# One counter for the activated x channels, one for the B and C rows of a Mamba block

## The chip, the cores and the metric

The kernel runs on one core of a Trainium2 chip. The metric is the time of one execution on the device in microseconds (us), as the median of several runs. Before the change: 3848.72 us, the median of 3 runs (3846.72 to 3849.55).

## What is computed

The input x is 64 batches of 256 x 256 float32. Two layers follow, each a graph attention and a feed-forward block, each on a layer norm of x and added to x.

```
x = x + L0_gnn(layernorm(x), adj)      # two dense layers, two attentions, ELUs
x = x + L0_ffn(layernorm(x))           # top-k routing, GELU, scatter back
x = x + L1_gnn(layernorm(x), adj)      # one masked attention, ELU
x = x + L1_ffn(layernorm(x))           # the Mamba block
```

The change lies in the Mamba block:

```
z, xBC, dt = split(x @ W_in)
xBC  = silu(conv_b + causal convolution of xBC over 4 taps)
xh, Bmat, Cmat = split(xBC, [512, 576])          # 512 x channels, 64 B rows, 64 C rows
xdt  = xh * dt                                   # dt = softplus(dt + dt_bias)
Y    = einsum(C, B, exp(segsum(dt * A)), xdt) + xh * D
Y    = Y * silu(z) ; RMS norm ; @ W_out @ W_lin + b_lin
```

## The kernel before

**Tiling.** All is float32. A batch is one 256 x 256 tile, held as two halves of 128 rows (U = 2). Matrices that go through TensorE are kept transposed, channels on partitions: the convolved channels are five tiles of 128 x 256 in `acc`, the first four (KI = 4) the 512 x channels, the fifth the 64 B rows and the 64 C rows. The eight PSUM banks are A0 to A2 (first attention), Q0, Q1 (router and second attention) and M0 to M2 (Mamba).

**Order of the work.** The 64 batches are pipelined. The table `STEPS` gives each of the five engines a written-out list of steps with a lag for each: in turn t a step of lag 5 works on batch t - 5. The prologue and the drain are unrolled, the turns between are one hardware loop. An engine does its instructions in order, and engines meet in semaphores alone, each of which is a counter: `then_inc(S["name"], 1)` on an instruction raises it when the instruction is done, `wait_ge(S["name"], b)` holds an engine's queue until the counter has reached b, the number of the batch.

**The place of the change.** The steps of the Mamba block that bear on it, with the engine and the lines:

- `m_silu` on ScalarE takes tanh of all five tiles of `acc` into `th` (L738). `m_silu` on VectorE then makes silu times two out of it, in three operations: L1010 for the four x tiles, in place (`xc` is another name of `acc`), L1012 for the B rows into `bT`, L1014 for the C rows into `cT`. The last one raises `xc_ready`.
- `m_xrow` on TensorE transposes `xc` back to rows, eight 128 x 128 transposes (L1339) into M2 and M0. ScalarE's `m_xrow` copies them to `xr` (L749), GpSimd's makes `xdt = xr * dt` (L564), which `m_y` on TensorE reads (L1353).
- `m_cb` on TensorE, right behind `m_xrow` in its list, multiplies `bT` and `cT` (L1332, L1333). VectorE masks the product into `cb` (L1030).
- `m_xbc_a` on ScalarE writes the first tap of the convolution of the next batch into `acc` (L708), and before that waits until the batch before is done with it (`before(act, S["xc_ready"], b)`).

On TensorE the list around it reads: `q_ffn1.1` (L1257), `a_mlp1.0` and `a_mlp1.1` (L1129, sixteen matmuls), `m_xrow`, `m_cb`, `a_fc.0` and `a_fc.1` (L1140), `q_ffn2` (L1264), a few small steps, `m_y` (L1353), `a_att` (L1160). On VectorE: ... `b_elu_c` (L904), `b_x1` (L921, L927), `q_gelu_a` (L963), `m_silu`, `g_x3` (L933), statistics, `m_cb` (L1030), `a_fc` (h, L807), `m_norm`, `q_ffn2` (L974, the GELU product, whose tanh is L704 on ScalarE). ScalarE's decays of the Mamba block are L760 and L764.

Of the kernel before, what the change touches and what calls it, by code (L numbers as in the profile page):

```python
# [7 lines left out]
ALU = mybir.AluOpType  # L8
# [36 lines left out]
def gnn_ffn_mamba_kernel(nc, x, adj, mlp1_w, mlp1_b, mlp2_w, mlp2_b, W_fc, a_fc, W_hand, a_hand,  # L45
# [24 lines left out]
    with ExitStack() as ctx:  # L70
# [6 lines left out]
        def sem(name):  # L77
            return ctx.enter_context(nc.semaphore(name))
# [141 lines left out]
        def rows1(half, u, extra=0):  # L220
# [13 lines left out]
            wsum_ready w_ps wrow_ready rank_ready pick_ready sel_ps sel_ready  # L234
            up_ps ga_ready gsq_ready gq_ready gt_ready gl_ready yff_ps yff_ready sc_ps xs_ready
            x2_ready x3_ready
            xbc_ps acc_ready conv th_ready xc_ready
            dt_ps dt_a_ready dt_abs dt_e_ready dt_chain dt_ready dA_ps cumT_ready cumc_ps cumcol_ready
            cb_ps cb_ready z_ps tz_ready gz_ready xr_ps xr_ready xdt_ready fall_ready dec0_ready dec1_ready mix_ready
            y_ps ysum yg_ready sq_ready sq_half yss_ready ss_ps ms_ready da_ready rms_ready out_ps x3b_ready x4_ready"""  # L240
        S = {name: sem(name) for name in NAMES.split()}
# [214 lines left out]
        def nth(b, per, i):  # L456

            return b * per - (per - i)

        def before(eng, semaphore, b):  # L460

            if not (isinstance(b, int) and b < 2):
                eng.wait_ge(semaphore, b - 1)
# [115 lines left out]
        def _(act):  # L579
# [126 lines left out]
            def first_tap(k, src):  # L706

                return nc.scalar.activation(acc[:, k, :], src, ACT.Identity, bias=c_conv[:, k:k + 1],  # L708
                                            scale=w_conv[:, k, PAD:PAD + 1])

            def m_xbc_a(b):
                before(act, S["xc_ready"], b)
                act.wait_ge(S["xbc_ps"], nth(b, 3, 1))
                first_tap(4, M1[:, N:2 * N])
                nc.scalar.copy(bc_in[:, PAD:], M1[:, N:2 * N]).then_inc(S["acc_ready"], 1)

                if not (isinstance(b, int) and b < 2):
                    act.wait_ge(S["ysum"], nth(b, 2, 0))
                act.wait_ge(S["xbc_ps"], nth(b, 3, 2))
                first_tap(0, M2[:, 0:N])  # L720
                first_tap(1, M2[:, N:]).then_inc(S["acc_ready"], 1)
# [44 lines left out]
            def m_gated(b):  # L766
# [8 lines left out]
                b_att=elu_exp("b", A2), g_att=elu_exp("g", Q1), b_elu_b=b_elu_b, g_elu=g_elu,  # L775
                q_route=q_route, q_gather=q_gather, q_gelu_a=q_gelu_a, q_gelu_c=q_gelu_c,
                m_xbc_a=m_xbc_a, m_xbc_b=m_xbc_b, m_dt_exp=m_dt_exp, m_silu=m_silu, m_z=m_z,
                **parts("m_decay", m_decay, 2), m_xrow=m_xrow, m_gated=m_gated))

        @block.vector  # L780
        def _(v):
# [224 lines left out]
            def m_silu(b):  # L1006

                v.wait_ge(S["th_ready"], b)
                c = acc
                nc.vector.scalar_tensor_tensor(out=xc[:, 0:KI, :], in0=th[:, 0:KI, :], scalar=1.0, in1=c[:, 0:KI, :],  # L1010
                                               op0=ALU.add, op1=ALU.mult)
                nc.vector.scalar_tensor_tensor(out=bT[:], in0=th[0:DS, KI, :], scalar=1.0, in1=c[0:DS, KI, :],  # L1012
                                               op0=ALU.add, op1=ALU.mult)
                nc.vector.scalar_tensor_tensor(out=cT[:], in0=th[DS:, KI, :], scalar=1.0, in1=c[DS:, KI, :],  # L1014
                                               op0=ALU.add, op1=ALU.mult).then_inc(S["xc_ready"], 1)

            def m_scan(b):
                v.wait_ge(S["dA_ps"], b)
# [60 lines left out]
            def m_out(b):  # L1079
# [17 lines left out]
                b_x1=b_x1, g_x3=g_x3, q_route=q_route, q_rank=q_rank,  # L1097
                q_gelu_a=q_gelu_a, q_gelu_b=q_gelu_b,
                q_ffn2=q_ffn2, q_scatter=q_scatter, q_x2=q_x2, **parts("m_conv_b", m_conv_b, PAD), m_silu=m_silu,
                m_scan=m_scan,  # L1100
                m_cum_col=m_cum_col, m_cb=m_cb, m_gate=m_gate,
# [3 lines left out]
        def _(pe):  # L1105
# [221 lines left out]
                last.then_inc(S["cumc_ps"], 1)  # L1327

            def m_cb(b):
                pe.wait_ge(S["xc_ready"], b)  # L1330
                pe.wait_ge(S["cumcol_ready"], b)
                nc.tensor.matmul(M1[:, 0:N], bT[:, 0:P], cT[:, :], start=True, stop=True)  # L1332
                nc.tensor.matmul(M1[:, N:N + P], bT[:, P:], cT[:, P:], start=True, stop=True).then_inc(S["cb_ps"], 1)  # L1333
# [31 lines left out]
            def m_out(b):  # L1365
# [14 lines left out]
                g_att=att("g", Q1), q_route=q_route, q_gather=q_gather, **parts("q_ffn1", q_ffn1, 2),  # L1380
                q_ffn2=q_ffn2, q_scatter=q_scatter, m_xbc_a=m_xbc_a, m_xbc_b=m_xbc_b, m_z=m_z, m_da=m_da,
                m_cum_col=m_cum_col, m_cb=m_cb, m_xrow=m_xrow, **parts("m_y", m_y, 2), m_dt=m_dt, m_ss=m_ss, m_out=m_out))


# [23 lines left out]
```

## Time and profile before

| | before |
|---|---|
| median of 3 runs | 3848.72 us (3846.72 to 3849.55) |
| profiled execution: its own time | 3847.21 us |
| its span, first to last instruction | 3845.5 us |
| PE (TensorE matmul) busy | 3658.6 us, 95% |
| PEld (TensorE weight load) busy | 3166.9 us, 82% |
| DVE (VectorE) busy | 2966.9 us, 77% |
| ACT (ScalarE) busy | 2364.6 us, 61% |
| POOL (GpSimd) busy | 997.1 us, 26% |
| mean granted TensorE clock | 0.983 of full speed |

The profile is of one execution. Its times count from the first instruction of the program. A busy share is an average over the whole span; PE's matmuls are pipelined, and the ends of their rows are modelled, so that a row of a group can reach a little into the next. "M<-ident,acc" is an instruction that writes a tile M from tiles ident and acc; "x8" are eight of them merged into one row. What stands in brackets at the end of a row is how long the engine was idle before it, and which instruction it waited for.

### The profile page before, as it was taken

The numbers are of one execution on the slowest core, as the hardware profiler recorded it, in microseconds if no ns is written. First come the engines' busy times: TensorE is split into PE (matmuls) and PEld (weight loads), VectorE is DVE, ScalarE is ACT, GpSimd is POOL, SyncE is SP. The second block draws the span as 40 slices with busy tenths as digits, with TensorE's granted clock in tenths as the row PEclk, the third lists the DMA queues.
The fourth block names the chain that finished last, engine by engine and source line by source line (L and its number), as shares of the span: only waits on it lengthen the run. The fifth ranks groups of instructions, "written<-read, shape, count | busy, mean of one in ns | idle before, by whom it ended". The sixth has DMA issues, their size and how long they took to land.

```text
span 3845.5 us, 63918 instructions
## 1 busy us (share of the span) xinstructions
PE 3658.6 (95%) x21016; PEld 3166.9 (82%) x21016; DVE 2966.9 (77%) x7731; ACT 2364.6 (61%) x5314; POOL 997.1 (26%) x1817
## 2 busy tenths in 40 slices
PE   2789999999999999999999999999999999999985
PEld 2578888888888888888888888888888888888864
DVE  2358887887887888788787888878878788887875
ACT  1246666666666666666666666666666666666654
POOL 0012223223223222322322222232232222223222
PEclk9889999999999999999999999999999999999987
DMA  3000010010011001001001100100100110010000
GB/s 93 11 23 28 30 38 27 30 38 27 30 38 38 27 30 38 27 30 38 28 29 38 38 27 30 38 27 30 38 27 30 38 38 27 30 38 27 31 28 31
DMA packets 73763, 126.85 MB, mean 33 GB/s; under 512 B 9984, under 2 KB 64128, under 8 KB 65536
## 3 DMA queue, kind: packets, MB, share of 16 engines
q1 hardware_dynamic: 73728, 126.42, 9.5%
q8 instruction: 18, 0.29, 0.0%
q14 instruction: 17, 0.14, 0.0%
HBM read 109.10 MB, written 17.30 MB: 33 GB/s over the span
## 4 chain that ended last, share of the span: by engine, by line
PE 75%; DVE 15%; ACT 5%; issue 3%; DVEq 0%; POOL 0%; DMA 0%; POOLq 0%
PE A L1140 12%; PE M L1276 7%; PE A L1160 6%; PE A L1178 6%; PE Q L1264 6%; PE M L1310 6%; PE M L1369 6%; PE A L1225 3%; PE A L1187 3%; PE Q L1187 3%; PE Q L1225 3%; DVE ga_ L963 2%; PE M L1339 2%; DVE acc L1010 2%; PE A L1170 2%
## 5 line engine op out<-in xcount | busy, mean ns | idle before, releaser
L1140 PE MATMUL A<-w_fc,o1T 128*128 128x256 f32 (+1 forms) x2048 | 460.9, 383 | 3.7 <-ACT o1T L591 3.7
L1140 PEld LDWEIGHTS A<-w_fc,o1T 128*128 128x128 f32 x2048 | 382.4, 189 | 65.1 <-ACT o1T L591 5.3
L507 POOL TENSOR_TENSOR var_m<-mv_m,epsilon 128x2 f32<-128x2 f32 x64 | 12.7, 198 | 1416.7 <-DVE mv_m L792 1416.7
L760 ACT ACTIVATE dec<-cumB,cumcol 128x256 f32<-128x256 f32 (+1 forms) x1024 | 366.2, 442 | 0.0
L1001 DVE SCALAR_TENSOR_TENSOR acc<-M,w_conv,acc 128x255 f32<-128x255 f32 (+2 forms) x768 | 314.5, 467 | 0.0
L1276 PE MATMUL M<-xT_m,w_in 128*128 128x256 f32 x1280 | 297.5, 379 | 0.8 <-DVE tz L1043 0.5
L1160 PE MATMUL A<-h,low 128*128 128x257 f32 (+1 forms) x1024 | 255.6, 393 | 22.4 <-DVE low L833 14.0
L1276 PEld LDWEIGHTS M<-xT_m,w_in 128*128 128x128 f32 x1280 | 237.7, 190 | 32.1 <-DVE tz L1043 2.0
L1257 PE MATMUL Q<-selT,w_up 128*128 128x128 f32 x2048 | 249.5, 275 | 0.9 <-ACT selT L696 0.9
L1043 DVE SCALAR_TENSOR_TENSOR tz<-tz,M 128x512 f32<-128x512 f32 x128 | 88.0, 687 | 205.7 <-ACT tz L743 205.7
L1178 PE MATMUL A<-e,w_mlp 128*128 128x256 f32 x1024 | 242.2, 391 | 1.5 <-DVE e L857 1.5
L1129 PE MATMUL A<-xT_a,w_mlp 128*128 128x256 f32 x1024 | 237.3, 386 | 3.8 <-DVE ue_b L921 3.1
L1264 PE MATMUL Q<-w_down,gsq 128*128 128x256 f32 x1024 | 234.6, 383 | 6.0 <-DVE gsq L974 6.0
L1257 PEld LDWEIGHTS Q<-selT,w_up 128*128 128x128 f32 x2048 | 238.8, 192 | 1.2 <-ACT selT L696 1.1
L1160 PEld LDWEIGHTS A<-h,low 128*128 128x128 f32 x1024 | 188.7, 194 | 60.7 <-DVE low L833 38.2
L1310 PE MATMUL M<-xT_m,w_in 128*128 128x256 f32 x1024 | 235.0, 383 | 0.0
L1369 PE MATMUL M<-w_comb,xr 128*128 128x256 f32 x1024 | 231.6, 379 | 3.4 <-DVE xr L1064 3.4
L564 POOL TENSOR_TENSOR xdt<-xr,dt 128x1024 f32<-128x1024 f32 x64 | 135.2, 2112 | 365.9 <-ACT xr L749 365.9
L708 ACT ACTIVATE acc<-M,c_conv,w_conv 128x256 f32<-128x256 f32 x320 | 168.4, 566 | 92.1 <-PE M L1276 92.1
L1264 PEld LDWEIGHTS Q<-w_down,gsq 128*128 128x128 f32 x1024 | 196.5, 192 | 34.0 <-DVE gsq L974 6.6
L1051 DVE TENSOR_TENSOR dec<-dec,cb 128x2048 f32<-128x2048 f32 (+1 forms) x128 | 223.5, 1747 | 0.1
L1369 PEld LDWEIGHTS M<-w_comb,xr 128*128 128x128 f32 x1024 | 194.1, 190 | 30.7 <-DVE xr L1064 3.9
(233 smaller groups left out, 8839.1 us busy)
## 6 DMA issues: line engine op xcount, KB each, us to landing
cumB<-cum_dram SPq DMA_DIRECT2D x64, 1024.0 KB, 4.7
x_in<-in_x SPq DMA_DIRECT2D x64, 256.0 KB, 2.8
x<-in_x SPq DMA_DIRECT2D x64, 256.0 KB, 2.9
out<-x3b SPq DMA_DIRECT2D x64, 256.0 KB, 2.8
w_mlp<-in_L_gnn_mlp_w SPq DMA_DIRECT2D x2, 512.0 KB, 5.6
w_fc<-in_L_gnn_W_fc SPq DMA_DIRECT2D x2, 512.0 KB, 6.3
w_up<-in_L_ffn_w SPq DMA_DIRECT2D x1, 1024.0 KB, 10.1
w_down<-in_L_ffn_w SPq DMA_DIRECT2D x1, 1024.0 KB, 11.2
```

The source lines that it names most:

```text
L760: last = nc.scalar.activation(dec[:, h, :], columns[:, h, :], ACT.Relu, bias=cumcol[:, i, h:h + 1], scale=-1.0)
L1001: last = nc.vector.scalar_tensor_tensor(out=acc[:, k, late:], in0=src, scalar=w_conv[:, k, tap:tap + 1], in1=acc[:, k, late:], op0=ALU.mul ...
L1129: last = nc.tensor.matmul(ps[:, (m - m0) * N:(m - m0 + 1) * N], w_mlp1[:, k, m * P:(m + 1) * P], xT["a"][:, k, :], start=(k == 0), stop=(k ...
L1140: last = nc.tensor.matmul(rows1(half, u, 2), o1T[:, k, u * P:(u + 1) * P], w_fc[:, k, half, 0:D + 2 * i], start=(k == 0), stop=(k == KH - 1))
L1160: last = nc.tensor.matmul(rows1(half, u, 1), p1[:, j, u * P:(u + 1) * P], h1[:, j, half, 0:D + 1 - half], start=(j == 0), stop=(j == U - 1))
L1178: last = nc.tensor.matmul(A1[:, m * N:(m + 1) * N], w_mlp2[:, k, m * P:(m + 1) * P], z1T[:, k, :], start=(k == 0), stop=(k == KH - 1))
L1187: last = nc.tensor.matmul(banks[u][:, 0:D + 2], src[:, c, u * P:(u + 1) * P], w[:, c, :], start=(c == 0), stop=(c == KD - 1))
L1257: last = nc.tensor.matmul(ps[:, (m - m0) * P:(m - m0 + 1) * P], w_up[:, c, m * P:(m + 1) * P], selT[:, c, :], start=(c == 0), stop=(c == K ...
L1264: last = nc.tensor.matmul(Q0[:, 0:D], gl[:, m, :], w_down[:, m, :], start=(m == 0), stop=(m == KF - 1))
L1276: last = nc.tensor.matmul(ps[:, at:at + N], w_in[:, c, X0 + k * P:X0 + (k + 1) * P], xT["m"][:, c, :], start=(c == 0), stop=(c == KD - 1))
L1310: last = nc.tensor.matmul(ps[:, (k - 2 * i) * N:(k - 2 * i + 1) * N], w_in[:, c, Z0 + k * P:Z0 + (k + 1) * P], xT["m"][:, c, :], start=(c ...
L1369: last = nc.tensor.matmul(M2[:, u * D:(u + 1) * D], yg[:, c, u * P:(u + 1) * P], w_comb[:, c, :], start=(c == 0), stop=(c == KI - 1))
```

## The change

The three operations of VectorE's `m_silu` get two counters in place of one. L1010, the one that makes the x channels, now raises `xc_ready`; L1014, the last one, raises a new counter `bc_ready`. TensorE's `m_xrow` keeps its wait for `xc_ready`, and so waits for L1010. TensorE's `m_cb` and ScalarE's `m_xbc_a` wait for `bc_ready`, that is for L1014 as before. No instruction is added, and the order on every engine is the same.

```diff
@@ NAMES
-            xbc_ps acc_ready conv th_ready xc_ready
+            xbc_ps acc_ready conv th_ready xc_ready bc_ready
@@ ScalarE
             def m_xbc_a(b):
-                before(act, S["xc_ready"], b)
+                before(act, S["bc_ready"], b)
@@ VectorE, m_silu
                 nc.vector.scalar_tensor_tensor(out=xc[:, 0:KI, :], in0=th[:, 0:KI, :], scalar=1.0, in1=c[:, 0:KI, :],
-                                               op0=ALU.add, op1=ALU.mult)
+                                               op0=ALU.add, op1=ALU.mult).then_inc(S["xc_ready"], 1)
                 nc.vector.scalar_tensor_tensor(out=bT[:], in0=th[0:DS, KI, :], scalar=1.0, in1=c[0:DS, KI, :],
                                                op0=ALU.add, op1=ALU.mult)
                 nc.vector.scalar_tensor_tensor(out=cT[:], in0=th[DS:, KI, :], scalar=1.0, in1=c[DS:, KI, :],
-                                               op0=ALU.add, op1=ALU.mult).then_inc(S["xc_ready"], 1)
+                                               op0=ALU.add, op1=ALU.mult).then_inc(S["bc_ready"], 1)
@@ TensorE
             def m_cb(b):
-                pe.wait_ge(S["xc_ready"], b)
+                pe.wait_ge(S["bc_ready"], b)
                 pe.wait_ge(S["cumcol_ready"], b)
```

## Rows read from the trace of the kernel before

**Rows 1.** The page: busy times, and the engines of the chain that ended last

```profile
PE 3658.6 (95%) x21016; PEld 3166.9 (82%) x21016; DVE 2966.9 (77%) x7731; ACT 2364.6 (61%) x5314; POOL 997.1 (26%) x1817
...
PE 75%; DVE 15%; ACT 5%; issue 3%; DVEq 0%; POOL 0%; DMA 0%; POOLq 0%
```

**Rows 2.** Waits (us, times, longest): whole span, then PE from 580 to 3620 us

```profile
PE M L1339 <- DVE cT L1014: 35.4, 61, 9.0
...
PE M L1339 <- DVE cT L1014: 10.6, 53, 0.2
```

**Rows 3.** Timeline of one steady batch (start us, duration us, engine, line, what, count)

```profile
1981.42 0.84 ACT L666 ACTIVATE ea_b<-A,rr_b 128x256 f32<-128x256 f32 x2 [0.81 <-PE A L1225]
...
1985.45 3.62 PE L1129 MATMUL A<-xT_a,w_mlp 128*128 128x256 f32 x16
...
1987.23 1.21 DVE L1010 SCALAR_TENSOR_TENSOR acc<-th,acc 128x1024 f32<-128x1024 f32 x1
...
1988.36 0.41 DVE L1012 SCALAR_TENSOR_TENSOR bT<-th,acc 64x256 f32<-64x256 f32 x1
1988.79 0.42 DVE L1014 SCALAR_TENSOR_TENSOR cT<-th,acc 64x256 f32<-64x256 f32 x1
1989.24 0.69 DVE L933 SCALAR_TENSOR_TENSOR x<-ue_g,x 128x512 f32<-128x512 f32 x1
1989.26 0.86 PEld L1339 LDWEIGHTS M<-ident,acc 128*128 128x128 f32 x8 [0.60 <-DVE cT L1014]
1989.26 1.10 PE L1339 MATMUL M<-ident,acc 128*128 128x128 f32 x8 [0.20 <-DVE cT L1014]
...
1990.29 0.70 PE L1332 MATMUL M<-cT,bT 64*128 64x256 f32 x2
```

**Rows 4.** Timeline of an unheld hand-over to transposes, earlier in the turn

```profile
1965.26 3.62 PE L1310 MATMUL M<-xT_m,w_in 128*128 128x256 f32 x16
...
1968.50 0.57 PEld L1214 LDWEIGHTS Q<-ident,sc_g 128*128 128x128 f32 x4
1968.71 0.60 PE L1214 MATMUL Q<-ident,sc_g 128*128 128x128 f32 x4
...
1969.15 0.38 PE L1187 MATMUL A<-w_hand,o2T 128*128 128x258 f32 x1
```

**Rows 5.** PE's timeline: first transpose of batches 30, 59 and 60 (cut)

```profile
1932.73 1.10 PE L1339 MATMUL M<-ident,acc 128*128 128x128 f32 x8 [0.20 <-DVE cT L1014]
...
3572.20 1.10 PE L1339 MATMUL M<-ident,acc 128*128 128x128 f32 x8 [0.20 <-DVE cT L1014]
...
3624.91 3.62 PE L1129 MATMUL A<-xT_a,w_mlp 128*128 128x256 f32 x16
3628.56 0.66 PE L1339 MATMUL M<-ident,acc 128*128 128x128 f32 x4
```

**Rows 6.** The drain: timeline of batch 63; last 245 us: busy, PEclk, DMA

```profile
3780.22 1.97 PE L1339 MATMUL M<-ident,acc 128*128 128x128 f32 x8 [8.71 <-DVE cT L1014]
...
3786.62 1.05 ACT L749 COPY xr<-M 128x512 f32<-128x512 f32 x2
...
3600.00:3845.00 245.00, 187.58 (x1024) 156.73 (x1022) 161.79 (x373) 126.70 (x276) 63.88 (x116) 0.87 0.08 30
```

**Rows 7.** Timeline of the same batch after `m_cb`: the next hand-overs to PE

```profile
1994.89 0.69 DVE L807 TENSOR_SCALAR h<-A 128x512 f32<-128x512 f32 x1 [0.59 <-PE A L1140]
1994.97 1.04 ACT L704 ACTIVATE gsq<-gsq 128x1024 f32<-128x1024 f32 x1
...
1996.15 1.22 DVE L974 SCALAR_TENSOR_TENSOR gsq<-gsq,ga_ 128x1024 f32<-128x1024 f32 x1
...
1997.96 3.43 PEld L1264 LDWEIGHTS Q<-w_down,gsq 128*128 128x128 f32 x16
...
2000.48 2.12 POOL L564 TENSOR_TENSOR xdt<-xr,dt 128x1024 f32<-128x1024 f32 x1 [5.53 <-ACT xr L749]
...
2003.46 2.82 PE L1353 MATMUL M<-dec,xdt 128*64 128x256 f32 x32
```

## The prediction

> **What bounds the kernel now.** I began with the page. TensorE (PE) is busy for 95% of the span and makes 75% of the chain of work that ended last, VectorE (DVE) 15% and ScalarE (ACT) 5% [rows 1]. So PE sets the pace, but in part of every batch the chain leaves it. The list of waits says where: between 580 and 3620 us PE waits for one thing only, the first row transpose of `m_xrow` (L1339) for the last of the three operations of VectorE's `m_silu` (L1014, cT), 53 times, 10.6 us in all, 0.2 us each [rows 2]. In the whole run there are 61 such waits, 35.4 us: 57 short ones (batches 3 to 59) and four long ones in the drain (61 to 64).
>
> Then the timeline of one batch [rows 3]. `m_silu` issues L1010 (xc: what the transposes read), L1012 (bT) and L1014 (cT), which only `m_cb` reads. xc ends at 1987.23 + 1.21 = 1988.44, cT at 1988.79 + 0.42 = 1989.21, and the first transpose starts at 1989.26, 0.05 after cT. The transposes thus wait 0.77 us for two results that they don't read. The work ahead of xc hangs on PE through ACT (ea_b waits for PE's L1225), so it does not move when PE gets faster after the transposes.
>
> **How much of it PE can take back.** PE can't gain 0.77 us per batch, since it is busy until just before. What it can gain is read from the starts of matmuls. A group of sixteen 256-column matmuls (L1310, start 1965.26) hands over to a group of transposes (L1214, start 1968.71) after 3.45 us [rows 4]. The sixteen of L1129 start at 1985.45, so an unheld first transpose would start at 1988.90; it starts at 1989.26: **0.36 us per batch**. xc with the same 0.05 us of signalling is there at 1988.49. Unheld, the weights of a transpose are loaded 0.21 us ahead of it (1968.50 for 1968.71), which here is 1988.69: still 0.20 after xc is ready, so this wait goes altogether.
>
> There is a second, small term. Held back, the transposes restart cold: weight load and matmul both start at 1989.26 [rows 3], not 0.21 apart. Four unheld transposes take 0.60, and four more move the end by 0.44 (1968.71 to 1969.15, rows 4), so eight take 1.04; L1339's eight take 1.10: **0.06 us per batch**.
>
> Two other prices can be read for the same wait. The idle time that the waits' list gives is 0.20, from the modelled end of the last matmul; the weight loads' own idle time is 0.60 [rows 3]. I take neither. The 0.60 contains the 0.21 that the load is normally ahead, and the 0.20 leaves out the overlap that matmuls in a stream have (the 3.62 us group is followed after 3.45). One row decides: batch 60 is held back less (L1129 starts at 3624.91, so the transpose is due at 3628.36; it starts at 3628.56, 0.20 late), and its transpose follows that of batch 59, which started at 3572.20, by 56.36 us, where the batch of rows 3 follows its neighbour by 56.53 (1989.26 after 1932.73) [rows 5]. Held back 0.16 us less, the batch came 0.17 us sooner. The starts tell what the kernel pays.
>
> The Trainium skill, page "Perfetto Trace Analysis", section "Tensor Engine Instruction (MATMUL, LD_WEIGHTS)", says that a matmul's start is recorded and its end computed from its size; by ends the gain would be an estimated 57 x 0.20 = 11 us, by starts it is the sum below.
>
> **The change, part by part.** No instruction is added, removed or moved; three of them signal or wait on another counter.
> - L1010 now raises a counter, and the transposes wait for it: 57 x (0.36 + 0.06) = 23.9 us for batches 3 to 59. Batches 1, 2 and 60 are held for 0.20 us and restart cold as well: 3 x (0.20 + 0.06) = 0.8 us. Together **24.7 us**.
> - The added update on L1010: no row shows this instruction with one. L1012 starts at 1988.36, 0.08 before L1010 ends. At best it costs nothing; at worst bT waits for L1010's end and a signal, 0.08 + 0.05 = 0.13 us. I take nothing, and 0.13 would be covered too (next point).
> - `m_cb` waits for the new counter behind cT. PE comes to it at 1990.29 - 0.42 = 1989.87, cT with its signal is there at 1989.26: 0.61 us of cover, so nothing.
> - ScalarE's `m_xbc_a` waits for the new counter of the batch before, raised by the same instruction as until now: nothing.
> - The four long waits of the drain: the transposes go 0.77 us sooner, and nobody takes it up. In batch 63 they start at 3780.22, but their copy on ACT (L749) starts only at 3786.62, behind the decays [rows 6]. In the other three the chain of waits passes by the transposes too, over the decays or over the VectorE operations after cT. Nothing, four times.
>
> **What is late next.** PE is then 0.42 us earlier against everything that hangs on work ahead of the transposes [rows 7]. VectorE's h (L807) waits 0.59 for PE today, 0.17 then. The GELU product: ACT's tanh (L704) ends at 1994.97 + 1.04 = 1996.01, L974 can follow at 1996.04 and ends at 1997.26; the weights of L1264 are due at 1997.96 - 0.42 = 1997.54, 0.28 of cover. xdt on GpSimd (POOL) ends at 2000.48 + 2.12 = 2002.60, L1353 is due at 2003.46 - 0.42 = 2003.04, 0.44 of cover. All hold, so the batch's period falls from 56.53 to about 56.11 us, with PE alone as its bound, apart from the wait for `low` at L1160, which hangs on PE's L1264 and moves with it.
>
> **The sum.** The profiled execution took 3847.21 us. 3847.2 - 24.7 = 3822.5. It lies 1.5 us under the median of the runs, 3848.72, so the forecast for the median is **3824.0 us**. A tenth of a microsecond less per batch (xdt or the product a little late) would be 3830; full use of the 0.60 can't be, as shown. In the last 245 us the granted clock is 0.87 [rows 6], and an earlier drain may meet its low stretches otherwise: a tenth of the missing 13% on 187.6 us of PE work is 2.4 us either way. The forecast's own range is 3820 to 3830.
>
> **The rivals.**
> - *Only the reported idle time comes back*, 0.20 us per batch: 3848.7 - 11.4 - 0.6 = 3837. For it speaks the waits' list, against it batch 60. Chance 0.05.
> - *The wait comes back later in the batch*, at h, at L1264 or at L1353. The covers of 0.17, 0.28 and 0.44 are small, and ends on POOL are rough. If one of them is wrong by its whole size and 0.42 more, nothing is gained: 3848.7; at half of that 3836. Chance 0.06, two thirds of it above the bound of no change.
> - *The transposes wait as before*, since xc is not signalled sooner than cT in practice: 3848.7. Against it: L1010 ends 0.77 before L1014. Chance 0.01.
> - *Slower: the update in the middle holds up VectorE.* Place: between L1010 and L1012. If it delayed bT and cT by X, `m_cb` would become PE's wait above X = 0.61, and the batch would be longer than today above 0.61 + 0.42 = 1.03 us. Held for as long as L1010 itself runs, 1.21, it costs 57 x 0.18 = 10 us: 3859. Against it: L1014 has an update today, and the next operation (L933, 1989.24) follows 0.03 after its end at 1989.21 [rows 3]. Chance 0.02.
>
> The last one has a rule on its side. The Trainium skill, "VectorE: DVE Perf Modes", section "The DRAIN you can't avoid", has the next VectorE operation wait until the pipeline is empty, and the update itself cost nothing extra. By that rule bT would start no sooner than L1010's end; the trace has it 0.08 sooner, and neither reaches the 1.03 us.
>
> **The numbers.** The forecast has 0.86, and its range with what lies just above it, 3820 to 3832, holds the time 8 times in 10. 0.2% (7.7 us) is about what a measurement of this kernel can tell from no change. Faster by more than that: the forecast, the first rival and the part of the second under it, 0.94; within it 0.04; slower 0.02.
>
> **What the profile after should show.** L1339 in the steady batches starts 3.45 us after L1129 and follows xc, not cT; the waits' list has no wait of PE there between 580 and 3620 us, and the weight load stands 0.2 us ahead; the eight take 1.04 us; the period is 56.11 us; h waits some 0.17 us; L1012 still starts before L1010's end. I am wrong if the period is above 56.2, or if a wait at L1264, L1353 or L1332 has taken the place of the one at L1339.

## The result, and the profile after

| | before | after |
|---|---|---|
| median of 6 runs each | 3848.56 us (3846.72 to 3849.55) | **3822.94 us** (3822.66 to 3825.32) |
| ratio to before, 95% interval | | 0.9936 (0.9923 to 0.9948) |
| profiled execution: own time, span | 3847.21, 3845.5 us | 3825.32, 3823.6 us |
| mean granted TensorE clock | 0.983 | 0.982 |
| period of a steady batch (first transpose to the next one's) | 56.53 us | 56.12 us |

The kernel is 25.6 us faster; 24.7 were forecast. The page of the kernel after, busy times and chain, against [rows 1]:

```profile
PE 3648.1 (95%) x21016; PEld 3173.2 (83%) x21016; DVE 2973.8 (78%) x7731; ACT 2366.6 (62%) x5314; POOL 986.6 (26%) x1817
...
PE 86%; DVE 8%; issue 2%; ACT 1%; POOL 0%; DVEq 0%; DMA 0%; POOLq 0%
```

The chain that ended last now runs over TensorE for 86% of the span instead of 75%, since in a steady batch it no longer steps over to VectorE at the transposes. The waits of TensorE in the whole run of the kernel after, against [rows 2] (columns: engine, where, awaited; us in total, times, longest):

```profile
PE M L1339 <- DVE acc L1010: 21.0, 4, 8.2
PE A L1160 <- DVE low L833: 14.2, 5, 4.1
```

Of 61 waits at L1339 the four of the drain are left, now for xc. The timeline of a steady batch of the kernel after, against [rows 3] (start, duration, what; another batch, so only distances compare):

```profile
1975.59 3.62 PE L1129 MATMUL A<-xT_a,w_mlp 128*128 128x256 f32 x16
...
1977.39 1.22 DVE L1010 SCALAR_TENSOR_TENSOR acc<-th,acc 128x1024 f32<-128x1024 f32 x1
...
1978.52 0.41 DVE L1012 SCALAR_TENSOR_TENSOR bT<-th,acc 64x256 f32<-64x256 f32 x1
1978.84 1.01 PEld L1339 LDWEIGHTS M<-ident,acc 128*128 128x128 f32 x8
1978.94 0.42 DVE L1014 SCALAR_TENSOR_TENSOR cT<-th,acc 64x256 f32<-64x256 f32 x1
1979.05 1.04 PE L1339 MATMUL M<-ident,acc 128*128 128x128 f32 x8
...
1980.02 0.70 PE L1332 MATMUL M<-cT,bT 64*128 64x256 f32 x2
```

The first transpose starts 3.46 us after L1129, where it was 3.81; its weights are loaded 0.21 ahead; the eight take 1.04 us. bT still starts 0.09 before xc ends. cT is ready at 1979.36 and `m_cb` starts at 1980.02. The next hand-overs of the same batch, against [rows 7]:

```profile
1984.62 0.69 DVE L807 TENSOR_SCALAR h<-A 128x512 f32<-128x512 f32 x1 [0.17 <-PE A L1140]
1985.13 1.04 ACT L704 ACTIVATE gsq<-gsq 128x1024 f32<-128x1024 f32 x1
1986.20 1.23 DVE L974 SCALAR_TENSOR_TENSOR gsq<-gsq,ga_ 128x1024 f32<-128x1024 f32 x1 [0.25 <-ACT gsq L704]
1987.68 3.43 PEld L1264 LDWEIGHTS Q<-w_down,gsq 128*128 128x128 f32 x16
...
1990.64 2.02 POOL L564 TENSOR_TENSOR xdt<-xr,dt 128x1024 f32<-128x1024 f32 x1 [5.55 <-ACT xr L749]
...
1993.19 1.09 PE L1353 MATMUL M<-dec,xdt 128*64 128x256 f32 x10
```

h waits 0.17; the GELU product ends 0.25 before the weights of L1264 are loaded, xdt 0.53 before L1353.

**Where the time went.** By starts, from the first transpose of batch 1 to that of batch 60: 3335.11 us before (293.45 to 3628.56), 3311.30 after (295.31 to 3606.61), 23.8 less. Of these, the 57 periods of batches 3 to 59 give 23.3, batch 2 0.25 and batch 60 0.24. The drain behind it takes 216.9 and 217.0. The prologue of this one profiled execution is 1.9 us longer, and it varies, from 293.1 to 295.3 over the kernels of the first five experiments. From some 55 us on, where the profile's record of the clock begins, it stands at the lower of its two levels (granted clock 0.50) for 68.3 us of the prologue before and for 75.1 after: 6.8 us more, which cost at most half as much, 3.4 us, and so can account for the 1.9. The profiled executions thus differ by 21.9 and the medians by 25.6; some 1.8 us between the medians are not located.

### The profile page after: what moved, and what is told of

It reads as the page before. It is cut to its first block, busy times and chain, and to the rows that moved or that the text cites. A ratio compares the mean times of both kernels' runs of the same rounds, so it can differ in the third digit from the quotient of the medians.

```text
span 3823.6 us, 63918 instructions
## 1 busy us (share of the span) xinstructions
PE 3648.1 (95%) x21016; PEld 3173.2 (83%) x21016; DVE 2973.8 (78%) x7731; ACT 2366.6 (62%) x5314; POOL 986.6 (26%) x1817
## 4 chain that ended last, share of the span: by engine, by line
PE 86%; DVE 8%; issue 2%; ACT 1%; POOL 0%; DVEq 0%; DMA 0%; POOLq 0%
PE A L1140 12%; PE M L1276 7%; PE A L1160 6%; PE A L1178 6%; PE A L1129 6%; PE Q L1264 6%; PE M L1310 6%; PE Q L1257 6%; PE M L1369 6%; PE A L1225 3%; PE A L1187 3%; PE Q L1187 3%; PE Q L1225 3%; PE A L1170 2%; PE M L1298 1%
## 5 line engine op out<-in xcount | busy, mean ns | idle before, releaser
L1140 PE MATMUL A<-w_fc,o1T 128*128 128x256 f32 (+1 forms) x2048 | 460.9, 383 | 3.7 <-ACT o1T L591 3.7
L1140 PEld LDWEIGHTS A<-w_fc,o1T 128*128 128x128 f32 x2048 | 382.5, 189 | 65.0 <-ACT o1T L591 5.3
L1160 PE MATMUL A<-h,low 128*128 128x257 f32 (+1 forms) x1024 | 256.9, 395 | 22.7 <-DVE low L833 14.2
L1264 PE MATMUL Q<-w_down,gsq 128*128 128x256 f32 x1024 | 234.7, 383 | 7.8 <-DVE gsq L974 7.8
L1129 PE MATMUL A<-xT_a,w_mlp 128*128 128x256 f32 x1024 | 236.6, 385 | 4.2 <-DVE ue_b L921 3.5
L1160 PEld LDWEIGHTS A<-h,low 128*128 128x128 f32 x1024 | 189.6, 195 | 61.4 <-DVE low L833 38.4
L1264 PEld LDWEIGHTS Q<-w_down,gsq 128*128 128x128 f32 x1024 | 196.6, 192 | 35.8 <-DVE gsq L974 8.4
L1178 PEld LDWEIGHTS A<-e,w_mlp 128*128 128x128 f32 x1024 | 194.2, 195 | 30.7 <-DVE e L857 2.7
```

The source lines that it names most:

```text
L1129: last = nc.tensor.matmul(ps[:, (m - m0) * N:(m - m0 + 1) * N], w_mlp1[:, k, m * P:(m + 1) * P], xT["a"][:, k, :], start=(k == 0), stop=(k ...
L1140: last = nc.tensor.matmul(rows1(half, u, 2), o1T[:, k, u * P:(u + 1) * P], w_fc[:, k, half, 0:D + 2 * i], start=(k == 0), stop=(k == KH - 1))
L1160: last = nc.tensor.matmul(rows1(half, u, 1), p1[:, j, u * P:(u + 1) * P], h1[:, j, half, 0:D + 1 - half], start=(j == 0), stop=(j == U - 1))
L1178: last = nc.tensor.matmul(A1[:, m * N:(m + 1) * N], w_mlp2[:, k, m * P:(m + 1) * P], z1T[:, k, :], start=(k == 0), stop=(k == KH - 1))
L1264: last = nc.tensor.matmul(Q0[:, 0:D], gl[:, m, :], w_down[:, m, :], start=(m == 0), stop=(m == KF - 1))
```

## The experiments

Theory: TensorE is paid by the starts of its matmuls, 0.42 us in each of 57 batches, and the transposes' wait has gone altogether. Rivals: a wait is left or has come back; the update on xc costs VectorE something. A start is called held when it comes later than in a stream without waits; the cover of a result is the time by which it is ready before it is due. Medians are of 4 runs unless told; "period" is the mean of batches 3 to 59.

### The transposes wait for bT as well

In the short diffs below, the three operations of VectorE's `m_silu` stand by the tiles that they write, with the counter that each raises.

```diff
-  xc (xc_ready) ; bT ; cT (bc_ready)
+  xc ; bT (xc_ready) ; cT (bc_ready)
```

> The kernel after the change, but the counter of the transposes is raised by L1012 (bT) instead of L1010 (xc): 0.33 us later, 0.44 us sooner than cT. Theory (PE pays from the start that is due to the start that comes, by the starts of the instructions): bT with its signal is there 0.08 us before the first transpose is due, but 0.13 us after its weights are. So the matmul comes on time, and only a restart cost of up to 0.06 us a batch is left: period 56.12 to 56.18 us, time 3823 to 3827 us. Rival (the gain goes with how early the signal comes): 0.33 of 0.77 us of the gain of 25.6 us is lost, 11 us: 3834 us.

Measured: 3824.30 us (3823.19 to 3824.86), ratio 0.9937 (0.992 to 0.9953), period 56.133 (56.124 after the change). The transposes follow L1129 after 3.46 us, as in the kernel after; their first weight load is only 0.075 us ahead instead of 0.214. So the transposes have at least this much room. The update on bT is not quite free: cT starts 0.032 us after bT's end, where without an update it is 0.014 (medians of the steady batches), and the three take 1.99 us instead of 1.98. The update on xc shows no such price, since bT starts 0.08 before xc's end with it and without it. The operation behind cT, which has had an update in the kernel before too, starts 0.031 after cT's end. The price of 0.02 us appears only where the next operation waits for the end of the one ahead, and it costs this kernel nothing.

### xc last, one counter

The kernel before, with the three operations in another order: bT, cT, xc, and one counter at xc.

```diff
-  xc ; bT ; cT (xc_ready)
+  bT ; cT ; xc (xc_ready)
```

> The kernel before the change with bT and cT made first and xc last, one counter raised by xc. Theory: the transposes truly wait for what they read now, but it is ready when cT was ready before, so nothing changes: period 56.53 us, time 3847 to 3850 us. Rival (the change gained because an update in the middle lets VectorE's or TensorE's queue run otherwise, or because waiting for an operation on 64 partitions is dear): 3840 us or less, since now the signal comes from L1010.

Measured: 3854.86 us (3852.70 to 3857.01, 10 runs), ratio 1.0018 (1.0008 to 1.0027), period 56.633. I had not expected the extra 6.7 us over the kernel before (3848.18 beside it). Its timeline:

```profile
1990.77 0.41 DVE L1010 SCALAR_TENSOR_TENSOR bT<-th,acc 64x256 f32<-64x256 f32 x1
1991.19 0.42 DVE L1012 SCALAR_TENSOR_TENSOR cT<-th,acc 64x256 f32<-64x256 f32 x1
1991.63 1.23 DVE L1014 SCALAR_TENSOR_TENSOR acc<-th,acc 128x1024 f32<-128x1024 f32 x1
1992.77 0.68 DVE L933 SCALAR_TENSOR_TENSOR x<-ue_g,x 128x512 f32<-128x512 f32 x1
1992.91 0.86 PEld L1339 LDWEIGHTS M<-ident,acc 128*128 128x128 f32 x8 [0.70 <-DVE acc L1014]
```

In [rows 3] bT starts 0.08 before xc ends, cT 0.02 after bT ends, and L933 0.03 after cT ends. Here cT starts 0.01 after bT, xc 0.02 after cT, and it is L933 that overlaps its predecessor, by 0.09. The overlap has moved behind the result that TensorE waits for, so the three end 2.09 us after their first start instead of 1.98: 57 x 0.10 = 5.7 us, which is nearly the miss. The operations that start only after the one ahead has ended are those beside cT, which alone reads partitions 64 to 127. The Trainium skill, "VectorE: DVE Perf Modes", section "Two Vector instructions with no wait between them", has a model for it: an instruction with an input or an output that starts in another group of 32 partitions than the first input or the output of the last one is held until every earlier one has finished. The four starts beside cT agree; no run here moves the partitions to test it by itself.

### B and C first, `m_cb` ahead of the transposes

```diff
@@ VectorE
-  xc (xc_ready) ; bT ; cT (bc_ready)
+  bT ; cT (bc_ready) ; xc (xc_ready)
@@ TensorE's list
-  ('m_xrow', 5), ('m_cb', 5)
+  ('m_cb', 5), ('m_xrow', 5)
```

> Another way to the same cover: bT and cT first with their counter, xc last with its own, and on TensorE m_cb ahead of m_xrow. The signals stand as they need to: bT and cT are ready 0.8 us before m_cb is due, and xc 0.49 us before the transposes are, which come 0.85 us later than now. Theory (only the wait at the place where PE has nothing to do counts): period 56.12 us, time 3821 to 3825 us, as after the change. Rival (the transposes' early start itself is what is gained, by xr and xdt): their 0.85 us later start would cost, 3830 us or more.

Measured: **3820.85 us** (3820.17 to 3822.48), ratio 0.9930 (0.9913 to 0.9947), period 56.078. This is 0.15 us below the range expected, and 0.047 us a batch less than after the change; no cost of the later transposes is seen. What it gains is in the starts next to `m_cb`, which works on 64 rows: behind it, after the change, L1140's second matmul starts 0.320 us after its first, and here, behind transposes, 0.219 (0.216 is the spacing of a stream). The second transpose, now behind `m_cb`, starts 0.164 after the first instead of 0.109. 0.101 - 0.055 = 0.046. The starts say where it is gained; that the 64 rows are the reason is argued, as no run changes the rows alone.

### Spare operations between xc and bT

One, two or three more operations of VectorE, each a copy of bT's into a tile that nobody reads:

```diff
-  xc (xc_ready) ; bT ; cT (bc_ready)
+  xc (xc_ready) ; spare 0 ; spare 1 ; spare 2 ; bT ; cT (bc_ready)
```

One: 

> The kernel after the change with one more VectorE operation of L1012's shape (0.42 us, into a spare tile) between xc and bT: xc is as early as now, bT and cT and all VectorE work behind them come 0.42 us later. Theory (m_cb has 0.60 us of cover, h and the GELU product 0.17 and 0.28 in a row): nothing, 3821 to 3825 us. Rival (the cover of 0.17 us at h is the real one, VectorE is nearly the bound): 57 x 0.25 = 14 us more, 3837 us.

Two: 

> Two such operations, 0.84 us. Theory: m_cb waits for 0.84 - 0.60 = 0.24 us and restarts cold (0.06): 57 x 0.24 to 0.30 = 14 to 17 us more, 3837 to 3840 us, and the waits' list shows PE L1332 waiting for L1014. Rival (VectorE is the bound from h on): 57 x 0.67 = 38 us more, 3861 us.

Three: 

> Three such operations, 1.26 us, beyond the 1.03 us from which the prediction's slower rival would have made the kernel slower than before. Theory: m_cb waits for 0.66 us and restarts cold: 57 x 0.66 to 0.72 = 38 to 41 us more, 3861 to 3864 us, slower than the kernel before. Rival (the place of the wait doesn't matter, only its sum with xc's): 3823 + 57 x (1.26 - 0.77) = 3851 us.

| spare operations | median, us | ratio (95%) | period | first matmul of `m_cb` after the last transpose |
|---|---|---|---|---|
| none (after) | 3822.94 | 0.9936 (0.9923 to 0.9948) | 56.124 | 0.203 |
| 1 | 3823.87 | 0.9937 (0.9920 to 0.9953) | 56.129 | 0.203 |
| 2 | 3826.85 | 0.9944 (0.9928 to 0.9961) | 56.173 | 0.267 |
| 3 (10 runs) | 3848.59 | 1.0001 (0.9991 to 1.0010) | 56.509 | 0.599 |

One is as expected. Two and three came out 10 to 13 and 12 to 15 us under the expectations. The timeline with three shows why:

```profile
1986.31 1.21 DVE L1011 SCALAR_TENSOR_TENSOR acc<-th,acc 128x1024 f32<-128x1024 f32 x1
1987.44 0.41 DVE L1013 SCALAR_TENSOR_TENSOR spare<-th,acc 64x256 f32<-64x256 f32 x1
...
1987.78 0.41 DVE L1015 SCALAR_TENSOR_TENSOR spare<-th,acc 64x256 f32<-64x256 f32 x1
...
1988.11 0.41 DVE L1017 SCALAR_TENSOR_TENSOR spare<-th,acc 64x256 f32<-64x256 f32 x1
1988.45 0.41 DVE L1019 SCALAR_TENSOR_TENSOR bT<-th,acc 64x256 f32<-64x256 f32 x1
1988.87 0.42 DVE L1021 SCALAR_TENSOR_TENSOR cT<-th,acc 64x256 f32<-64x256 f32 x1
...
1989.35 0.70 PE L1339 MATMUL M<-cT,bT 64*128 64x256 f32 x2 [0.33 <-DVE cT L1021]
```

Each spare operation lasts 0.41, but the operation behind it starts 0.33 or 0.34 after it, so the delays are 0.33, 0.67 and 1.0, not multiples of 0.42. Against a cover of 0.60 that leaves nothing, 0.07 and 0.40, and the held starts of the table are 0, 0.064 and 0.396. So the cover of `m_cb` is measured, and so is the rival's point: a delay of 1.0 gives back the whole gain (0.02 us of period are left).

### Spare operations ahead of xc

Two of the same, in front of xc, which delays all three.

```diff
-  xc (xc_ready) ; bT ; cT (bc_ready)
+  spare 0 ; spare 1 ; xc (xc_ready) ; bT ; cT (bc_ready)
```

> The kernel after the change with two more VectorE operations of L1012's shape (0.41 to 0.42 us each, into a spare tile) ahead of xc: xc, bT and cT come 0.84 us later. Theory: xc with its signal comes 0.43 us after the transpose is due, and restarts it cold for 0.06 us: 57 x 0.49 = 28 us more than 3823: 3851 us, period 56.61 us; VectorE's own 54 us more of work cost nothing beside that. Rival (VectorE's work between its waits is bound as well): 57 x 0.84 = 48 us more, 3871 us. Rival (covers larger than read): under 3840 us.

Measured: 3844.04 us (3841.38 to 3845.68, 10 runs), ratio 0.9989 (0.9979 to 0.9998), period 56.433; 7 us under the expectation. Two rows of it:

```profile
1986.20 1.21 DVE L1015 SCALAR_TENSOR_TENSOR acc<-th,acc 128x1024 f32<-128x1024 f32 x1
...
1987.46 0.86 PEld L1344 LDWEIGHTS M<-ident,acc 128*128 128x128 f32 x8 [0.50 <-DVE acc L1015]
```

xc is 0.67 us late, not 0.84 (the first spare starts at 1985.53). Its end and 0.05 of signal are at 1987.46, where the load starts. The first transpose starts 0.262 later behind L1129 than unheld and its second 0.06 later than in a stream: 0.32, and the period grew by 0.31. Room for the transposes is thus about 0.67 - 0.26 = 0.41: the 0.20 to the load and the 0.21 by which the load goes ahead. With e1, where xc's signal comes with bT's end, 0.33 us later, it agrees: no wait.

### The next wait in line: `low` in halves

After the change the next place in a steady batch where TensorE is held is L1160, by `low`:

```profile
1995.25 0.85 DVE L833 SCALAR_TENSOR_TENSOR low<-fac,bcol,low 128x256 f32<-128x256 f32 x2
...
1996.15 1.60 PEld L1160 LDWEIGHTS A<-h,low 128*128 128x128 f32 x8 [0.38 <-DVE low L833]
```

There the two operations of VectorE's L833 now signal one by one, and TensorE takes the four matmuls of the first half in the order in which their inputs come.

```diff
@@ VectorE, L833, in the loop over the two halves
-                last.then_inc(S["p1_ready"], 1)
+                    last.then_inc(S["p1_ready"], 1)
@@ TensorE, a_att
-                pe.wait_ge(S["p1_ready"], b)
+                pe.wait_ge(S["p1_ready"], nth(b, 2, 1 + half))
+  (u, j) in the order (0,0) (1,0) | wait for the second | (0,1) (1,1)
```

> The same cut at the place where PE still waits in each batch: L1160 starts 0.41 us after the group before it and 0.30 us after it is due, for the second of the two operations of L833 that make p1. Now each raises the counter, and the first two matmuls, one for either half of the rows, take the first half of p1 alone. Theory: the wait of 0.30 us and the cold restart of 0.10 us go, the next thing that could be late is the second layer norm (xn_g) for the transposes of g_turn, with its weights held for up to 0.1 us: 57 x 0.35 to 0.40 = 20 to 23 us less than after the change, 3800 to 3803 us, period about 55.75 us. Rival (the waits' list is right that PE waits for nothing there now, since it lists 0.2 us in all): 3823 us. Rival (something anchored ahead of L1160 takes over at once, as xn_g): 3812 us or more.

Measured: 3826.16 us (3825.64 to 3826.99), ratio 0.9944 (0.9928 to 0.9961), period 56.115: nothing gained. The wait did shrink: the first matmul there follows the one ahead after 0.203 us, where it was 0.415. But the transposes of u (L1171 here, behind L849) went from 0.112 to 0.316:

```profile
2003.99 1.66 DVE L849 SCALAR_TENSOR_TENSOR u<-A,r,e 128x256 f32<-128x256 f32 x4
...
2005.13 0.50 PE L1363 MATMUL M<-ones,yss 128*128 128x1 f32 x4
...
2005.70 0.85 PEld L1171 LDWEIGHTS A<-ident,u 128*128 128x128 f32 x8
```

u ends at 2005.65 and the transposes start 0.05 later. The wait has moved one step on, as the last rival had it, only at u. TensorE's gain did get as far as VectorE: seen from the first transpose of the batch, VectorE's L1069, four operations ahead of u, starts at 22.98 us instead of 23.19 (medians of the steady batches). But it takes 1.11 us instead of 0.89 and ends at 24.09 in both, and u behind it ends at 26.81 and 26.82. In both it overlaps an operation of GpSimd (L516), which has not moved and ends at 23.54. After the change, then with `low` in halves, and last in the drain of the kernel after, where GpSimd does nothing meanwhile:

```profile
2001.30 1.29 POOL L516 TENSOR_TENSOR xs<-x,xn_q 128x512 f32<-128x512 f32 x1 [4.65 <-DVE xn_q L800]
2002.24 0.90 DVE L1069 TENSOR_TENSOR th<-th 128x512 f32<-128x512 f32 x1
```

```profile
2001.07 1.30 POOL L516 TENSOR_TENSOR xs<-x,xn_q 128x512 f32<-128x512 f32 x1 [4.65 <-DVE xn_q L800]
2001.80 1.12 DVE L1069 TENSOR_TENSOR th<-th 128x512 f32<-128x512 f32 x1
```

```profile
3732.02 0.69 DVE L1069 TENSOR_TENSOR th<-th 128x512 f32<-128x512 f32 x1 [0.48 <-ACT th L768]
```

Wherever L1069 starts in L516, it ends 0.55 after it (2003.14 and 2002.59; 2002.92 and 2002.37). So it is to 0.01 us in the 61 batches of every kernel here in which the two overlap, and in one of the drain it starts 0.4 after L516 does and lasts 1.45. By these rows what holds u is the operation of GpSimd, and starting L1069 sooner gives nothing while the two overlap. No run moved L516 to test it.

### u in halves as well, with a step of VectorE moved

L849 goes by halves and signals each; TensorE transposes half by half; and on VectorE the mask of the second attention (`g_mask`) moves behind `m_ms` and `a_uturn`.

```diff
-  ('a_elu_c', 2), ('g_mask', 4), ('m_ms', 6), ('a_uturn', 2),
+  ('a_elu_c', 2), ('m_ms', 6), ('a_uturn', 2), ('g_mask', 4),
@@ TensorE, a_uturn
-                pe.wait_ge(S["u1_ready"], b)
-                for ps, c0 in ((A2, 0), (A0, 2)):
+                for ps, c0 in ((A0, 0), (A2, 2)):
+                    pe.wait_ge(S["u1_ready"], nth(b, 2, 1 + c0 // 2))
```

> The wait that moved in the run with p1 in halves is handled too: u (L849) is made half by half and signalled twice a batch, TensorE transposes each half on its own signal, VectorE adds each half (L857) as it comes, and VectorE's mask of the second attention moves behind that. In the run with p1 in halves the first transpose of u started 0.316 us after the matmul ahead of it, where 0.112 is its pitch unheld: 0.204 held, and about 0.06 for the cold restart. Theory (the matmul's start can follow its own half of u, and no other VectorE result is late at once): period 56.115 - 0.26 = 55.85 us, the median about 3808, range 3803 to 3813. Rival (the next step that hangs on VectorE, the masks of the second attention that now come 1.3 us later, or the sum behind L857, takes over at once): period 56.1 or more, 3821 to 3835.

With B and C first besides: 

> The same with the B and C rows made first and m_cb ahead of the transposes, which took 0.047 us off the period by itself. Theory (the two gains are in different places of the turn and add up): 57 x 0.047 = 2.7 us less than the run without it, about 3805. Rival (TensorE is held by a VectorE result on the way between them, so that the second gain only lengthens that wait): the same time as the run without it, within 1 us.

Measured: 3894.33 us (3893.48 to 3894.81), ratio 1.0122 (1.0106 to 1.0139), and with B and C first 3916.23 (3893.47 to 3932.25), 1.0159 (1.0112 to 1.0207). The transposes of u are unheld, but the step that I had moved is needed: TensorE's next transposes into the bank that the mask reads (L1109, wsum) wait for it. From the first of the two kernels:

```profile
2040.20 0.86 DVE L875 SCALAR_TENSOR_TENSOR sc_g<-mask,fc_g,Q 128x256 f32<-128x256 f32 x2
...
2041.21 0.40 PE L1109 MATMUL Q<-ident,wsum 128*128 128x128 f32 x2 [1.10 <-DVE sc_g L875]
```

1.10 us are listed as idle in each batch, and by starts the transposes are held for 1.24 (1.356 behind the matmul ahead instead of 0.112): the rival that named the mask, and worse than it was priced. Part of the price is the clock: of the 57 periods of batches 3 to 59 in the profiled execution 44 are 57.0 us and 13 are 58.5 to 58.7. The second kernel's spread goes with the same, as told in the last section; that kernel decides nothing about B and C first.

### u and the sum behind it in halves, no step moved

```diff
@@ `low` and u in halves as before, VectorE's list as after the change
@@ VectorE, a_uturn: z1_ready raised by each of the two operations
@@ TensorE, a_mlp2
-                pe.wait_ge(S["z1_ready"], b)
+                        if m == 0 and k in (0, 2):
+                            pe.wait_ge(S["z1_ready"], nth(b, 2, 1 + k // 2))
```

> The halves of u again, but with VectorE's list left as it was (the mask ahead of L857), since the moved mask made the turn of wsum wait 1.24 us in the run before; and the sum behind the transposes (L857) signals each half, so that the first eight matmuls behind it (L1179) wait for its first half and only the third of them for the second. In the run with p1 in halves L857 starts at 2006.41 right behind the mask, its halves end near 2007.05 and 2007.69; L1179 started at 2007.77 and would be due at 2007.51. Theory (both halves of that hand-over are ready, nothing else is late at once): period 56.115 - 0.26 = 55.85 us, the median about 3811, range 3807 to 3815. Rival (another step that hangs on VectorE takes over again): the wait appears at a named matmul between L1171 and the next L1339 and the time stays at 3821 to 3828.

With B and C first besides: 

> The same with the B and C rows made first and m_cb ahead of the transposes, which alone took 0.047 us off the period. Theory: the gains are in different places of the turn and add up, 57 x 0.047 = 2.7 us under the run without it, about 3808. Rival: something that hangs on VectorE stands between them and eats it: within 1 us of the run without it.

| | median, us | ratio (95%) | period | first transpose of batch 1 at |
|---|---|---|---|---|
| `low` in halves | 3826.16 | 0.9944 (0.9928 to 0.9961) | 56.115 | 295.37 |
| u and the sum too | 3807.76 (3805.45 to 3808.57) | 0.9896 (0.9879 to 0.9912) | 56.042 | 281.63 |
| and B and C first | **3803.17** (3802.45 to 3805.20) | 0.9885 (0.9868 to 0.9901) | 55.987 | 282.95 |

The median hits the expectation and the reason does not. The period fell by 0.07, not 0.26: 57 x 0.07 = 4 us of the 18. The rival's part is right again, at `m_dt` (L1301), which waits until `ms` (L1077) has read its bank, and `ms` stands behind the mask:

```profile
1989.64 1.07 PE L1172 MATMUL A<-ident,u 128*128 128x128 f32 x8
1989.70 0.86 DVE L875 SCALAR_TENSOR_TENSOR sc_g<-mask,fc_g,Q 128x256 f32<-128x256 f32 x2
1990.48 0.15 DVE L1077 TENSOR_SCALAR ms<-M 128x2 f32<-128x2 f32 x1
...
1990.77 1.03 PE L1301 MATMUL M<-w_in,xT_m 128*128 128x8 f32 x8
```

L1301 follows the last transpose after 0.34 us, where 0.11 is the pitch unheld. Seen from the first transpose of the batch it starts at 27.81 us with `low` in halves and here: the halves of u gave nothing. The 0.07 came from the halves of the sum. Of the sixteen matmuls behind it (L1181 here) the second now starts 0.218 us after the first instead of 0.291, and the sixteen take 3.456 us from first start to the next group instead of 3.528. The profiled executions differ by 20.2 us: 4.3 in the 59 periods from batch 1 to batch 60, 2.2 in the drain, and 13.7 ahead of the first transpose of batch 1, in the prologue, which I had not looked at. So the median came out as expected by luck. What is seen in the prologue is the granted clock: with `low` in halves, and then here (columns as in [rows 6]; the granted clock is the third from the right):

```profile
150.00:200.00 50.00, 40.70 (x183) 33.78 (x184) 20.64 (x61) 13.11 (x31) 3.81 (x6) 0.85 0.04 11
200.00:250.00 50.00, 43.18 (x205) 35.44 (x204) 23.71 (x70) 18.79 (x44) 3.90 (x7) 0.88 0.04 11
```

```profile
150.00:200.00 50.00, 39.51 (x199) 32.75 (x198) 22.26 (x69) 17.29 (x38) 5.09 (x7) 0.94 0.03 11
200.00:250.00 50.00, 41.98 (x211) 34.80 (x212) 26.21 (x81) 21.29 (x50) 5.08 (x9) 0.94 0.03 11
```

The clock goes from 0.85 and 0.88 to 0.94. Over the whole prologue it stands at the lower level for 75.1 us with `low` in halves and for 51.2 here. If TensorE had been busy all through the 23.9 us between them, the full clock would have saved half of it, 12 us; this is an upper bound. How much of the 13.7 us is shorter steps and how much is clock was not separated. B and C first adds 0.055 a batch, 57 x 0.055 = 3.1 us of the 4.6 between the medians, about as much as alone. This is the fastest of the kernels, 19.8 us under the change.

## Why the prediction was right

- **What bounds the kernel**: right. The one wait of the steady batches was the one that set their period.
- **0.36 us held, read from starts**: right. L1129 to the first transpose went from 3.81 to 3.46 us, forecast 3.45. Two spares ahead of xc held it by 0.26 again, and the period followed.
- **0.06 us for the cold restart**: right. The second transpose follows the first after 0.109 us instead of 0.168. Together 56.533 - 56.124 = 0.41 of 0.42; the rival with the idle time of the list, 0.20, is out.
- **The 57 steady batches, and batches 1, 2 and 60**: 23.3 for 23.9, and 0.25 and 0.24 for 0.26 each at batches 2 and 60. That of batch 1 lies in the prologue, whose spread hides it.
- **The update at no cost**: right on xc. On bT it delays cT by 0.02 us, which the cover hides.
- **`m_cb` covered by 0.61**: measured 0.60, by two spare operations that exceed it by 0.07 and three by 0.40.
- **The room of the transposes**, put at 0.20 us to the weight load, holds, but it is not the point from which it costs: the load's own lead of 0.21 goes first. With xc's signal at bT's end the lead shrinks to 0.075 and no matmul starts later. Two spares ahead of xc show 0.41 in all.
- **The drain gives nothing**: right, 216.9 and 217.0 us.
- **What is late next**: h waits 0.17 as forecast, the product has 0.25 of cover for 0.28, xdt 0.53 for 0.44. L1160 moved with TensorE, as said.
- **The slower rival's point, 1.03 us of delay for cT**: three spares delay it by 1.0 and the time is that of before, 3848.59. Its premise, that the update on xc holds up bT, is out.

The median of the forecast was 1.1 us high. The profiled execution of after is 2.4 us above the median of its kernel where that of before was 1.5 under its own; what is left of the difference is such spread. The chances are added up 0.01 off: the forecast, the first rival and the part of the second under 0.2% make 0.93, not 0.94, and with the third rival 0.05 lie within 0.2%.

The rule of the Trainium skill that the prediction named beside the slower rival, "VectorE: DVE Perf Modes", section "The DRAIN you can't avoid", was read too strictly: the same section says that an operation that is not held starts earlier. The trace has bT start 0.09 before xc's end, which agrees with that sentence.

## What to carry to other kernels

On an engine that works in order, a wait is worth the shift in the starts behind it, plus what a cold restart costs, and not the idle time that is listed; a neighbouring batch that is held less is the check on it. Signal each consumer from the operation that makes its input, and before reckoning with a gain, list the covers of everything behind that hangs on other engines: here the waits at `low` and at u were removed, and one close behind took over each time, so that 0.01 us and nothing came back; only a short wait inside a group, at the halves of the sum, gave its 0.07. A step that looks free to move on its own engine may be what frees a bank for another.

## What the runs showed of the hardware that I had not expected

- **The order of three VectorE operations changes their length.** With the operation on partitions 64 to 127 last, xc, bT and cT take 1.98 us from first start to last end; with it in the middle 2.09. Operations with the same partitions follow each other 0.33 us apart though each lasts 0.41.
- **An operation of VectorE that overlaps one of GpSimd can stand still.** L1069 lasts 0.69 us alone, and 0.90, 1.11 or 1.45 when it starts 0.34, 0.56 or 0.9 before the end of GpSimd's L516: it always ends 0.55 after it.
- **`m_cb`, a matmul over 64 rows between others, costs at both edges.** `m_cb` starts 0.203 us after the last transpose, where a transpose is followed after 0.109, and the second matmul of L1140 after it 0.320 instead of 0.216. No run changes the number of rows alone.
- **A short idle stretch can cost the clock.** In the kernel with the mask moved and B and C first, TensorE idles 1.10 us in every batch. In 23 of 57 periods nothing more follows; then the period is 56.9 us. In 34 it is 58.5 or 58.6. One of these (windows of 2 us; columns as in [rows 6]: length, busy time of PE, PEld, DVE, ACT and POOL, granted clock, DMA share, GB/s):

```profile
1478.00:1480.00 2.00, 0.98 (x4) 0.93 (x5) 1.97 (x7) 0.29 (x2) 0.00 (x0) 0.72 0.00 0
1480.00:1482.00 2.00, 2.00 (x6) 1.58 (x5) 2.00 (x5) 1.84 (x9) 1.02 (x2) 0.50 0.13 15
```

The granted clock of 0.50 is 1.2 GHz, and it came right behind the idle 1.10 us. In all 34 such batches here, and in all 13 of the kernel with the mask moved alone, the clock falls within half a microsecond of the end of that wait, and between batches 3 and 59 it falls nowhere else. The group of sixteen matmuls behind it in that batch, and in one of 56.9 us (the timelines of both):

```profile
1479.47 5.01 PE L1180 MATMUL A<-e,w_mlp 128*128 128x256 f32 x16
```

```profile
1537.79 3.62 PE L1180 MATMUL A<-e,w_mlp 128*128 128x256 f32 x16
```

So the same wait of 1.10 us can cost 1.4 us more in this group and 1.6 in the batch, and the spread of the four runs of this kernel, 39 us, goes with it: 3893.47 us at a mean granted clock of 0.976, 3900.49 at 0.974, 3931.98 and 3932.25 at 0.966, where all kernels without that wait have 0.98 or more. The waits of 0.2 and 0.4 us of the kernels before and after never did this: from 600 to 3600 us their granted clock is full. What decides in which batch the clock falls was not tested.
